# Head attention: maxima in two-row transfers, scans that lead by 24, and the first heads' positions inside the first blocks

## The chip, the core and the metric
The kernel runs on one core of a Trainium2 chip. The metric is the device time of one execution in microseconds, as the median of several runs. The engines are TensorE (PE: matmuls, with PEld for weight loads), VectorE (DVE), ScalarE (ACT), GpSimd (POOL) and SyncE (SP, which only issues transfers here).

## What is computed
The reference is a "macaron" block on 4096 tokens of 256 features, x of shape (2, 2048, 256):

```python
x = x + 0.5 * ffn(layernorm(x))     # three tree-routed feed-forwards, then attention over them
x = x + att(layernorm(x))           # 16 heads, what this change is about
x = x + 0.5 * ffn(layernorm(x))
# att, with 32 groups n = (batch, head slice), each 2048 rows of d_head 16:
att = softmax(einsum('nqd,nkd->nqk', qm, km))
att_out = einsum('nqk,nkd->nqd', att + batch_pos, vm)   # batch_pos: a relative bias table per head
```

So attention here has two products with the values: one with the softmax, one with `batch_pos`, which depends only on the head and the distance of the positions.

## The kernel before
The program is a row of stages. Those of head attention are `head_project` (q, k, v and their parts), `head_attend` (which the change is in) and `head_close`.

`head_attend` works through 32 blocks (BLOCKS), a block being one batch and head slice of 2048 rows. A block has two units (u = 2n and 2n + 1), each for half of the queries. A unit has 16 steps (RC), c = 0 to 15.

*Scans.* To know each query's maximum before the exponential, TensorE first computes all scores of a unit with queries as rows (`scan`, 32 matmuls of 48x512 a unit, into four PSUM banks `s1_ps`). VectorE takes maxima over two of them at once (`scan_max`), then forms the negative maximum of each query, splits it in two float32r parts (a cast and a subtraction) and transposes them (`max_parts`, four pieces put behind the first four scan maxima of the next unit). SP copies the transposed rows into the two last rows of the query stack `qs` (`load_m`), so that the score matmul subtracts the maximum itself.

*Scores.* `score` computes scores with keys as rows (50x512, the 50 being 48 rows and the two parts), ScalarE takes the exponential from PSUM (three turns of `s2_ps`, counted in `turn_of`), and `products` multiplies them by the values two steps (LATE) later. The ones column in the values gives the sum of the softmax.

*Order.* TensorE's order is written out in `step`: in each step two scans and two scores alternate, then follow the eight matmuls of `products`. The scans run ahead of the scores by one unit less four scans: LEAD is 14 steps of two, 28 scans, so a unit's last scans are made in step c = 1 of the unit before it. Before the first step stand all 32 scans of unit 0 and 28 of unit 1, with no other work beside them.

*Turn.* At the end of block n, VectorE transposes the block's output from PSUM and takes reciprocals of the sums (`turn_out`, in its own order behind scan maximum `TURN_AT` of an odd unit); TensorE waits for that before it writes `o_ps` again. On this GpSimd starts `finish`: it multiplies by the reciprocal, adds the position part and stores the block; then it issues the next loads (`load_pos`, `load_v`), places the values (`place_v`), and prepares a head two ahead (`prepare_above` in even, `prepare_below` in odd blocks: one 128x512 multiply, 15 small dependent adds, then casts and subtractions).

*Positions.* `positions(h, half)` is a burst of 11 matmuls for a head, in a turn of `s2_ps`; ScalarE copies it out (`copy_positions`), SP stores it (`store_pos`) and GpSimd loads it back for `finish`. Head 0 is done in the prologue, between scans of unit 1; head h + 1 in the second step (POS_AT = 1) of the even units of head h's blocks.

*Waits.* Each step of a unit that begins waits for `m_loaded` (all its `load_m` transfers), a block's first for its loads and for `v_placed`.

Of the kernel before, what the change touches and what calls it, by code (L numbers as in the profile page):

```python
# [34 lines left out]
PARTS = 2  # L35
# [1183 lines left out]
def head_attend(nc, tag, stacks, scan_loaded, ones_set, parts_d, v_d, table_d, skew_d, pos_d, att_d):  # L1219
# [3 lines left out]
    with ExitStack() as ctx:  # L1223
# [17 lines left out]
        UNIT = RC * PAIR  # L1241
        SCANS = UC * QG
        RING = 2 * SLOTS
        LEAD, LATE = 14, 2
        BANKS, TURNS = 4, 3
        QUADS = P // COLS
        HALF = 512 // 2
# [42 lines left out]
        stored = sem("att_stored")  # L1290
        LOADS = 2 * TERMS
        HEAD_LOADS = 3 + B
        MLOADS = QUADS * PARTS
        MSTEPS = 3
        FSTEPS = 2
        BELOW_STEPS, ABOVE_STEPS = RC + 4, RC + 5
        SUMS = BELOW_STEPS + ABOVE_STEPS

        turn_of = {}
        for half in range(2):  # L1300
            turn_of["pos", 0, half] = len(turn_of)
        for n in range(BLOCKS):
            for u in (2 * n, 2 * n + 1):
                for c in range(RC):
                    for g in range(PAIR):
                        turn_of["score", u, PAIR * c + g] = len(turn_of)
                    if c == POS_AT and u % 2 == 0 and n // 2 + 1 < HEADS:
                        turn_of["pos", n // 2 + 1, n % 2] = len(turn_of)

        def scores_done(n):  # L1310
            return turn_of["score", 2 * n + 1, UNIT - 1] + 1
# [15 lines left out]
        def _(sp):  # L1327
            def load_m(u):
                k = u // 2 % SLOTS
                sp.wait_ge(mT_made, u + 1)  # L1330
                for i in range(QUADS):
                    for part in range(PARTS):
                        row = LOW + QKROWS + part
                        at = i * COLS + part * UC
                        sp.dma_start(qs[row:row + 1, k, half_of(u), i * COLS:(i + 1) * COLS].bitcast(F32),
                                     mT[at:at + UC, u % 2, :]).then_inc(m_loaded, 16)

            def skew(h):
                sp.dma_start(skew_d[h], table_d[h:h + 1, :].broadcast_to([P, TABLE])).then_inc(skewed, 16)
# [24 lines left out]
            load_head(1)  # L1364
            load_m(0)
            load_head(2)
            for half in range(2):
                store_pos(0, half)
            for n in range(BLOCKS):
                if n > 0:  # L1370
                    sp.wait_ge(s2_made, scores_done(n - 1))
                if n + 2 < BLOCKS:
                    load_qk(sp, parts_d, stacks, n + 2, 0, scan_loaded)
                if n // 2 + 1 < HEADS:
                    store_pos(n // 2 + 1, n % 2)
                load_m(2 * n + 1)
                if n + 2 < BLOCKS:
                    load_qk(sp, parts_d, stacks, n + 2, LOW, score_loaded)
                if n % 2 == 0 and n // 2 + SLOTS < HEADS:
                    load_head(n // 2 + SLOTS)  # L1380
                    if n // 2 + SLOTS + 1 < HEADS:
                        skew(n // 2 + SLOTS + 1)
                if n + 1 < BLOCKS:
                    load_m(2 * n + 2)
            for k in range(2):
# [3 lines left out]
        def _(pool):  # L1389
# [75 lines left out]
            prepare_below(1)  # L1465
            prepare_above(1)
            prepare_below(2)
            load_pos(0)
            for n in range(BLOCKS):
                if n + 2 < BLOCKS:  # L1470
                    pool.wait_ge(v_placed, n + 1)
                    load_v(n + 2)
                if n + 1 < BLOCKS:
                    if n > 0:
                        pool.wait_ge(o_made, n)
                    place_v(n + 1)
                ahead = (n + 5) // 2
                if ahead < HEADS:
                    (prepare_below, prepare_above)[(n + 1) % 2](ahead)
                finish(n)  # L1480
                if n + 1 < BLOCKS:
                    load_pos(n + 1)
# [3 lines left out]
        def _(pe):  # L1486
# [52 lines left out]
            def step(u):  # L1539
# [5 lines left out]
                for c in range(RC):  # L1545
                    ahead = PAIR * (c + LEAD)
                    to, e = u + 1 + ahead // SCANS, ahead % SCANS
                    if to % 2 == 0 and e == 0 and to < UNITS:
                        pe.wait_ge(scan_loaded[to // 2 % SLOTS], 16 * LOADS * (to // 2 // SLOTS + 1))
                    for k in range(PAIR):  # L1550
                        if to < UNITS:
                            scan(to, e + k)
                        score(u, c, k)
                    if c >= LATE:
                        if c == LATE and u % 2 == 0 and n > 0:
                            pe.wait_ge(turn_step, 2 * n - 1)
                        products(u, c - LATE)
                    elif u > 0:
                        products(u - 1, RC + c - LATE)
                    if c == POS_AT and u % 2 == 0 and n // 2 + 1 < HEADS:  # L1560
                        positions(n // 2 + 1, n % 2)

            pe.wait_ge(scan_loaded[0], 16 * LOADS)
            for e in range(SCANS):
                scan(0, e)
            pe.wait_ge(constants_set, 4)
            for e in range(LEAD * PAIR):
                if e in (8, 16):
                    positions(0, e // 8 - 1)
                scan(1, e)  # L1570
            for u in range(UNITS):
                step(u)
# [57 lines left out]
        def _(act):  # L1630
# [6 lines left out]
                nc.scalar.copy(pos[:, half, groups, :].rearrange("p g w -> p (g w)"),  # L1637
                               s2_ps[:, turn % TURNS, 0:RC * W // 2]).then_inc(s2_free, 1)

            for half in range(2):  # L1640
                copy_positions(0, half)
            for u in range(UNITS):
                n = u // 2
                for i in range(UNIT):
# [2 lines left out]
                    act.wait_ge(s2_made, turn + 1)  # L1647
                    nc.scalar.activation(probs[:, (RC * u + c) % (LATE + 1), 4 * g:4 * g + 4, :].rearrange("p c t -> p (c t)"),  # L1648
                                         s2_ps[:, turn % TURNS, :], ACT.Exp).then_inc(s2_free, 1)
                    if c == POS_AT and g == PAIR - 1 and u % 2 == 0 and n // 2 + 1 < HEADS:  # L1650
                        copy_positions(n // 2 + 1, n % 2)


def head_close(nc, tag, w, att_d, y_d, x_in, x_out):
# [425 lines left out]
```

## Time and profile before

| | |
|---|---|
| median of 3 runs | 3017.08 us (3011.81 to 3024.38) |
| the profiled execution, its own time | 3022.94 us |
| its span, first to last instruction | 3021.1 us |
| TensorE busy in the span | 2805.2 us (93%) |
| VectorE busy | 2143.6 us (71%) |
| ScalarE busy | 1800.7 us (60%) |
| GpSimd busy | 801.5 us (27%) |
| mean granted TensorE clock | 0.961 |
| head attention, first scan to last product | 808 to 2174 us |

The busy shares are over all stages, which have different limits. A busy TensorE is not one at its peak, since the ends of matmuls are modelled. Times in the timelines count from the start of the span. "Idle before" is how long the engine stood still before a group, with the one that released it. In the trace the PSUM tiles s1_ps and s2_ps are both shown as `s_ps_ha`: line 1492 is the scan, line 1504 the score, line 1529 the positions.

### The profile page before, as it was taken

Reading aid. Unit: us, or ns where it says so; the run is one execution under the profiler, and the core shown is the slowest. Engines: PE = TensorE matmul, PEld = TensorE weight load, DVE = VectorE, ACT = ScalarE, POOL = GpSimd, SP = SyncE. Lnnn points to the kernel's source line nnn. Section 1 sums busy time; section 2 is a strip of 40 time slices with the busy share of each in tenths; the row PEclk is TensorE's granted clock in tenths of the full one; section 3 lists DMA queues with packets and bytes.
Section 4 is the critical chain, followed back from the end, with each engine's and each line's share of the span. In section 5 each row is a group of like instructions: output and inputs, shape, how many; then the busy total and the mean of one; then the engine's idle time right before and its main releaser. Section 6 shows DMA issues by size and latency. Waiting matters only on the chain. (4 is left out here: it accounts for less than half of the span.)

```text
span 3021.1 us, 57357 instructions
## 1 busy us (share of the span) xinstructions
PE 2805.2 (93%) x21096; PEld 1725.5 (57%) x21096; DVE 2143.6 (71%) x3412; ACT 1800.7 (60%) x3507; POOL 801.5 (27%) x1290
## 2 busy tenths in 40 slices
PE   4998999998799999999999999999786699899999
PEld 2877888886543333333333333333253377788888
DVE  5545555445589999999999999999344555555554
ACT  3445343335268888888888888888633355443333
POOL 4652300002352233322333222300012564320000
PEclk8999999998789999999999999999997799999999
DMA  8994211106954454454555454442043699221100
GB/s 261 292 303 126 67 31 32 32 23 221 263 68 61 59 69 63 55 67 58 63 68 68 59 66 53 55 57 33 13 158 113 187 306 304 74 60 32 32 27 21
DMA packets 442366, 302.17 MB, mean 100 GB/s; under 512 B 167768, under 2 KB 418748, under 8 KB 442092
## 3 DMA queue, kind: packets, MB, share of 16 engines
q1 hardware_dynamic: 413292, 214.59, 34.9%
q0 software_dynamic: 28800, 83.92, 8.9%
q8 instruction: 173, 2.83, 0.4%
q14 instruction: 101, 0.83, 0.1%
HBM read 183.27 MB, written 118.78 MB: 100 GB/s over the span
## 5 line engine op out<-in xcount | busy, mean ns | idle before, releaser
L1581 DVE TENSOR_REDUCE mx_ha<-s_ps_ha 128x2 f32<-128x1024 f32 x1024 | 1237.8, 1219 | 32.0 <-PE s_ps_ha L1492 27.3
L1648 ACT ACTIVATE probs_ha<-s_ps_ha 128x512 f32<-128x512 f32 x2048 | 1111.7, 595 | 169.0 <-PE s_ps_ha L1504 25.1
L1492 PE MATMUL s_ps_ha<-ks_ha,qs_ha 48*128 48x512 f32 x2048 | 760.7, 452 | 23.9 <-DVE mx_ha L1581 14.2
L1504 PE MATMUL s_ps_ha<-qs_ha,ks_ha 50*128 50x512 f32 x2048 | 747.9, 445 | 0.0
L1513 PE MATMUL o_ps_ha<-probs_ha,vs_ha 128*32 128x256 f32 x8192 | 654.1, 391 | 1.4 <-DVE oT_ha L1609 1.4
L1492 PEld LDWEIGHTS s_ps_ha<-ks_ha,qs_ha 48*128 48x128 f32 x2048 | 308.4, 188 | 444.9 <-DVE mx_ha L1581 388.7
L908 ACT ACTIVATE probsT_a<-pT_ps_a 128x512 fp32r<-128x512 f32 x256 | 146.3, 597 | 422.6 <-PE pT_ps_a L778 422.6
L1513 PEld LDWEIGHTS o_ps_ha<-probs_ha,vs_ha 128*32 128x32 f32 x8192 | 161.2, 108 | 375.6 <-ACT probs_ha L1648 352.0
L1504 PEld LDWEIGHTS s_ps_ha<-qs_ha,ks_ha 50*128 50x128 f32 x2048 | 302.0, 185 | 12.4 <-ACT probs_ha L1648 11.9
L1444 POOL TENSOR_TENSOR onorm_ha<-oT_ha,rinv_ha 128x256 f32<-128x256 f32 x32 | 19.9, 623 | 929.8 <-DVE rinv_ha L1612 929.8
L821 DVE TENSOR_REDUCE nmax_a<-s_ps_a 128x1 f32<-128x2048 f32 x64 | 146.7, 2292 | 155.3 <-PE s_ps_a L767 155.3
L728 POOL DMA_INDIRECT rows_a<-ys_d,slots x96 | 90.7, 945 | 620.0 <-PE turn_ps_a L750 572.1
L449 DVE COPY y_p<-y_ps_p 128x256 f32<-128x256 f32 x282 | 119.5, 424 | 190.2 <-PE y_ps_p L591 152.1
L253 POOL DMA_INDIRECT xs_d<-xn_p,row_of_p x192 | 186.2, 970 | 165.9 <-PE xT_ps_p L555 68.9
L481 ACT ACTIVATE h_p<-h_ps_p,wa_p 65x128 f32<-65x128 f32 x282 | 102.3, 363 | 170.8 <-PE h_ps_p L581 166.9
L767 PE MATMUL s_ps_a<-k0T_a,qT_a 128*128 128x512 f32 x768 | 202.2, 408 | 0.0
L581 PE MATMUL h_ps_p<-xsT_p,wa_p 128*65 128x128 f32 x1128 | 175.3, 278 | 25.2 <-issue 19.9
L767 PE MATMUL s_ps_a<-k1T,qT_a 128*128 128x512 f32 x768 | 190.4, 398 | 0.0
L800 PE MATMUL o_ps_a<-v_a,probsT_a 128*128 128x512 f32 x512 | 188.8, 408 | 0.0
L800 PE MATMUL o_ps_a<-v,probsT_a 128*128 128x512 f32 x512 | 188.5, 408 | 0.0
L581 PEld LDWEIGHTS h_ps_p<-xsT_p,wa_p 128*65 128x65 f32 x1128 | 134.6, 139 | 70.7 <-issue 37.9
L591 PE MATMUL y_ps_p<-leaf_w_p,h_p 65*128 x564 | 171.7, 386 | 0.6 <-issue 0.5
(221 smaller groups left out, 3884.0 us busy)
## 6 DMA issues: line engine op xcount, KB each, us to landing
xs_p<-xs_d SPq DMA_DIRECT2D x282, 128.0 KB
ys_d<-y_p SPq DMA_DIRECT2D x66, 512.0 KB
qs_ha<-parts_d SPq DMA_DIRECT2D x192, 128.0 KB, 4.5
ks_ha<-parts_d SPq DMA_DIRECT2D x192, 128.0 KB, 5.1
parts_d<-parts_hp POOLq DMA_DIRECT2D x32, 512.0 KB, 7.6
qs_ha<-mT_ha SPq DMA_DIRECT2D x512, 1.0 KB
xs_d<-y_p SPq DMA_DIRECT2D x6, 1024.0 KB, 12.4
leaf_w_p<-in_wa SPq DMA_DIRECT2D x4, 1048.0 KB
```

Of the source, the lines that this page charges most:

```text
L253: pool.indirect_dma_start(xs_d[f], bass.IndirectOffsetOnAxis(row_of[:, f, t:t + 1], 0), xn[:, t, :], None).then_inc(scattered[f], 16)
L581: last = nc.tensor.matmul(h_ps[0:W1C, n % 2, 0:P], wa[:, n % WB, c * W1C:(c + 1) * W1C], xsT[:, n % 2, c, :], start=(c == 0), stop=(c == C ...
L591: nc.tensor.matmul(y_ps[:, n % 2, 0:D], h[:, n % 2], leaf_w[0:W1C, n // SEG % 2, bass.ds(at + LA, D)], start=True, stop=True).then_inc(y_m ...
L767: last = nc.tensor.matmul(s_ps[:, g, :], qT[:, i % 2, hq, c, :], kT[b][:, hk, c, g * 512:(g + 1) * 512], start=(c == 0 and n == 0), stop=( ...
L800: nc.tensor.matmul(o_ps[:, :], probsT[:, 0, g, k * P:(k + 1) * P], value.rearrange("p h d -> p (h d)"), start=first, stop=False)
L821: nc.vector.reduce_max(nmax[:, :], s_ps[:, :, :].rearrange("p a b -> p (a b)"), AX_X, negate=True).then_inc(max_done, 1)
L908: nc.scalar.activation(probsT[:, 0, g, :], pT_ps[:, g % 2, :], ACT.Identity).then_inc(pT_high, 1)
L1492: nc.tensor.matmul(s1_ps[:, e % BANKS, :], qs[0:QKROWS, k, c, :], ks[0:QKROWS, k, g * 4:(g + 1) * 4, :].rearrange("p c t -> p (c t)"), sta ...
L1504: nc.tensor.matmul(out, ks[LOW:LOW + KR, k, c, :], qs[LOW:LOW + KR, k, first:first + 4, :].rearrange("p c t -> p (c t)"), start=True, stop ...
L1513: last = nc.tensor.matmul(out, vs[:, u // 2 % SLOTS, c, :], probs[:, (RC * u + c) % (LATE + 1), :, i * COLS:(i + 1) * COLS], start=(c == 0 ...
L1581: nc.vector.reduce_max(mx[:, at:at + 2], s1_ps[:, e % BANKS:e % BANKS + 2, :], AX_X).then_inc(s1_free, 1)
L1648: nc.scalar.activation(probs[:, (RC * u + c) % (LATE + 1), 4 * g:4 * g + 4, :].rearrange("p c t -> p (c t)"), s2_ps[:, turn % TURNS, :], A ...
```

## The change
LEAD goes from 14 to 12, so that scans lead by 24: 24 scans of unit 1 stand in the prologue, and a unit's last scans are made in step c = 3 of the unit before. `TURN_AT`, which is computed from it, goes from 30 to 26. `load_m` copies both parts of a quadrant in one transfer of two rows (16 source partitions), four in place of eight. The positions of head 0 leave the prologue; `pos_of` puts head 0 in units 0 and 1, head 1 in units 2 and 3, and the later heads where they were. SP stores the position halves in that order, and GpSimd's `load_pos(0)` comes behind its first preparations in block 0.

```diff
--- before.py
+++ after.py
@@ -1241,7 +1241,7 @@
         UNIT = RC * PAIR
         SCANS = UC * QG
         RING = 2 * SLOTS
-        LEAD, LATE = 14, 2
+        LEAD, LATE = 12, 2
         BANKS, TURNS = 4, 3
         QUADS = P // COLS
         HALF = 512 // 2
@@ -1290,22 +1290,25 @@
         stored = sem("att_stored")
         LOADS = 2 * TERMS
         HEAD_LOADS = 3 + B
-        MLOADS = QUADS * PARTS
+        MLOADS = QUADS
         MSTEPS = 3
         FSTEPS = 2
         BELOW_STEPS, ABOVE_STEPS = RC + 4, RC + 5
         SUMS = BELOW_STEPS + ABOVE_STEPS
 
+        def pos_of(u):
+            if u < 4:
+                return u // 2, u % 2
+            return (u // 4 + 1, u // 2 % 2) if u % 2 == 0 and u // 4 + 1 < HEADS else None
+
         turn_of = {}
-        for half in range(2):
-            turn_of["pos", 0, half] = len(turn_of)
         for n in range(BLOCKS):
             for u in (2 * n, 2 * n + 1):
                 for c in range(RC):
                     for g in range(PAIR):
                         turn_of["score", u, PAIR * c + g] = len(turn_of)
-                    if c == POS_AT and u % 2 == 0 and n // 2 + 1 < HEADS:
-                        turn_of["pos", n // 2 + 1, n % 2] = len(turn_of)
+                    if c == POS_AT and pos_of(u):
+                        turn_of["pos", *pos_of(u)] = len(turn_of)
 
         def scores_done(n):
             return turn_of["score", 2 * n + 1, UNIT - 1] + 1
@@ -1328,12 +1331,11 @@
             def load_m(u):
                 k = u // 2 % SLOTS
                 sp.wait_ge(mT_made, u + 1)
+                row = LOW + QKROWS
                 for i in range(QUADS):
-                    for part in range(PARTS):
-                        row = LOW + QKROWS + part
-                        at = i * COLS + part * UC
-                        sp.dma_start(qs[row:row + 1, k, half_of(u), i * COLS:(i + 1) * COLS].bitcast(F32),
-                                     mT[at:at + UC, u % 2, :]).then_inc(m_loaded, 16)
+                    at = i * COLS
+                    sp.dma_start(qs[row:row + PARTS, k, half_of(u), i * COLS:(i + 1) * COLS].bitcast(F32),
+                                 mT[at:at + PARTS * UC, u % 2, :]).then_inc(m_loaded, 16)
 
             def skew(h):
                 sp.dma_start(skew_d[h], table_d[h:h + 1, :].broadcast_to([P, TABLE])).then_inc(skewed, 16)
@@ -1364,15 +1366,13 @@
             load_head(1)
             load_m(0)
             load_head(2)
-            for half in range(2):
-                store_pos(0, half)
             for n in range(BLOCKS):
                 if n > 0:
                     sp.wait_ge(s2_made, scores_done(n - 1))
                 if n + 2 < BLOCKS:
                     load_qk(sp, parts_d, stacks, n + 2, 0, scan_loaded)
-                if n // 2 + 1 < HEADS:
-                    store_pos(n // 2 + 1, n % 2)
+                if pos_of(2 * n):
+                    store_pos(*pos_of(2 * n))
                 load_m(2 * n + 1)
                 if n + 2 < BLOCKS:
                     load_qk(sp, parts_d, stacks, n + 2, LOW, score_loaded)
@@ -1380,6 +1380,8 @@
                     load_head(n // 2 + SLOTS)
                     if n // 2 + SLOTS + 1 < HEADS:
                         skew(n // 2 + SLOTS + 1)
+                if pos_of(2 * n + 1):
+                    store_pos(*pos_of(2 * n + 1))
                 if n + 1 < BLOCKS:
                     load_m(2 * n + 2)
             for k in range(2):
@@ -1465,7 +1467,6 @@
             prepare_below(1)
             prepare_above(1)
             prepare_below(2)
-            load_pos(0)
             for n in range(BLOCKS):
                 if n + 2 < BLOCKS:
                     pool.wait_ge(v_placed, n + 1)
@@ -1477,6 +1478,8 @@
                 ahead = (n + 5) // 2
                 if ahead < HEADS:
                     (prepare_below, prepare_above)[(n + 1) % 2](ahead)
+                if n == 0:
+                    load_pos(0)
                 finish(n)
                 if n + 1 < BLOCKS:
                     load_pos(n + 1)
@@ -1557,16 +1560,14 @@
                         products(u, c - LATE)
                     elif u > 0:
                         products(u - 1, RC + c - LATE)
-                    if c == POS_AT and u % 2 == 0 and n // 2 + 1 < HEADS:
-                        positions(n // 2 + 1, n % 2)
+                    if c == POS_AT and pos_of(u):
+                        positions(*pos_of(u))
 
             pe.wait_ge(scan_loaded[0], 16 * LOADS)
             for e in range(SCANS):
                 scan(0, e)
             pe.wait_ge(constants_set, 4)
             for e in range(LEAD * PAIR):
-                if e in (8, 16):
-                    positions(0, e // 8 - 1)
                 scan(1, e)
             for u in range(UNITS):
                 step(u)
@@ -1637,8 +1638,6 @@
                 nc.scalar.copy(pos[:, half, groups, :].rearrange("p g w -> p (g w)"),
                                s2_ps[:, turn % TURNS, 0:RC * W // 2]).then_inc(s2_free, 1)
 
-            for half in range(2):
-                copy_positions(0, half)
             for u in range(UNITS):
                 n = u // 2
                 for i in range(UNIT):
@@ -1647,8 +1646,8 @@
                     act.wait_ge(s2_made, turn + 1)
                     nc.scalar.activation(probs[:, (RC * u + c) % (LATE + 1), 4 * g:4 * g + 4, :].rearrange("p c t -> p (c t)"),
                                          s2_ps[:, turn % TURNS, :], ACT.Exp).then_inc(s2_free, 1)
-                    if c == POS_AT and g == PAIR - 1 and u % 2 == 0 and n // 2 + 1 < HEADS:
-                        copy_positions(n // 2 + 1, n % 2)
+                    if c == POS_AT and g == PAIR - 1 and pos_of(u):
+                        copy_positions(*pos_of(u))
 
 
 def head_close(nc, tag, w, att_d, y_d, x_in, x_out):
```

## Rows read from the trace of the kernel before

**Rows 1.** Timeline of TensorE in an ordinary block: start us, duration us, engine, line, operands.
```profile
1599.75 1.31 PE L1529 MATMUL s_ps_ha<-vpp_ha,bandp_ha 128*128 128x256 f32 x9
1601.23 0.49 PE L1492 MATMUL s_ps_ha<-ks_ha,qs_ha 48*128 48x512 f32 x1
1601.89 0.64 PE L1513 MATMUL o_ps_ha<-probs_ha,vs_ha 128*32 128x256 f32 x8
...
1606.82 0.64 PE L1513 MATMUL o_ps_ha<-probs_ha,vs_ha 128*32 128x256 f32 x8
1608.53 0.64 PE L1513 MATMUL o_ps_ha<-probs_ha,vs_ha 128*32 128x256 f32 x8
...
1618.97 0.50 PE L1504 MATMUL s_ps_ha<-qs_ha,ks_ha 50*128 50x512 f32 x1
```

**Rows 2.** The page's costliest groups, the exponentials: busy us, mean ns | idle before.
```profile
L1648 ACT ACTIVATE probs_ha<-s_ps_ha 128x512 f32<-128x512 f32 x2048 | 1111.7, 595 | 169.0 <-PE s_ps_ha L1504 25.1
```

**Rows 3.** Timeline of VectorE and GpSimd in the same block.
```profile
1604.34 0.55 POOL L1391 DMA_DIRECT2D vflat_ha<-vh_d  x1
1604.37 0.57 DVE L1592 CAST mparts_ha<-nmax_ha 128x8 fp32r<-128x8 f32 x1
1604.85 1.21 DVE L1581 TENSOR_REDUCE mx_ha<-s_ps_ha 128x2 f32<-128x1024 f32 x1
1605.59 1.05 POOL L1412 TENSOR_TENSOR above_ha<-vp_ha,far_ha 128x512 f32<-128x512 f32 x1
1605.99 0.69 DVE L1595 TENSOR_TENSOR mparts_ha<-nmax_ha,mparts_ha 128x8 fp32r<-128x8 f32 x1
1606.72 4.87 POOL L1416 TENSOR_TENSOR above_ha<-above_ha 128x32 f32<-128x32 f32 x15
```

**Rows 4.** Groups of max_parts on VectorE: duration ns min/median/max.
```profile
L1588 DVE TENSOR_REDUCE nmax_ha<-mx_ha x64: 129/175/178, 830.7 to 2136.9; 128x8 f32<-128x32 f32 x64
L1592 DVE CAST mparts_ha<-nmax_ha x64: 159/163/580, 831.9 to 2137.0; 128x8 fp32r<-128x8 f32 x64
L1595 DVE TENSOR_TENSOR mparts_ha<-nmax_ha,mparts_ha x64: 149/157/1230, 833.5 to 2137.2; 128x8 fp32r<-128x8 f32 x64
```

**Rows 5.** Timeline, block beginnings early and late; then GpSimd's groups, 900 to 2100 us.
```profile
1601.50 0.62 POOL L1444 TENSOR_TENSOR onorm_ha<-oT_ha,rinv_ha 128x256 f32<-128x256 f32 x1 [27.87 <-DVE rinv_ha L1612]
...
1642.91 0.62 POOL L1444 TENSOR_TENSOR onorm_ha<-oT_ha,rinv_ha 128x256 f32<-128x256 f32 x1 [27.84 <-DVE rinv_ha L1612]
...
2014.92 0.62 POOL L1444 TENSOR_TENSOR onorm_ha<-oT_ha,rinv_ha 128x256 f32<-128x256 f32 x1 [36.79 <-DVE rinv_ha L1612]
...
2017.79 0.58 DVE L1592 CAST mparts_ha<-nmax_ha 128x8 fp32r<-128x8 f32 x1
2019.41 0.15 DVE L1595 TENSOR_TENSOR mparts_ha<-nmax_ha,mparts_ha 128x8 fp32r<-128x8 f32 x1
...
2055.86 0.62 POOL L1444 TENSOR_TENSOR onorm_ha<-oT_ha,rinv_ha 128x256 f32<-128x256 f32 x1 [36.80 <-DVE rinv_ha L1612]
...
L1412 POOL TENSOR_TENSOR below_ha<-vp_ha,far_ha 128x512 f32<-128x512 f32 x13 | 13.7, 1051 | 0.0
```

**Rows 6.** Windows: us, busy us of each engine, granted clock (PEclk), DMA share, GB/s.
```profile
856.00:857.00 1.00, 1.00 (x7) 0.55 (x6) 0.00 (x0) 0.37 (x1) 0.77 (x4) 0.74 0.00 0
```

**Rows 7.** Timeline of TensorE, prologue of head attention.
```profile
830.79 2.44 PE L1492 MATMUL s_ps_ha<-ks_ha,qs_ha 48*128 48x512 f32 x4 [0.25 <-DVE mx_ha L1581]
...
836.46 2.07 PE L1492 MATMUL s_ps_ha<-ks_ha,qs_ha 48*128 48x512 f32 x4
...
838.99 2.35 PE L1492 MATMUL s_ps_ha<-ks_ha,qs_ha 48*128 48x512 f32 x4 [0.46 <-DVE mx_ha L1581]
...
851.61 0.76 PE L1492 MATMUL s_ps_ha<-ks_ha,qs_ha 48*128 48x512 f32 x1 [0.28 <-DVE mx_ha L1581]
```

**Rows 8.** Timeline of SP's queue; then the page's DMA issues: KB, us to landing.
```profile
835.06 5.53 SPq L1335 DMA_DIRECT2D qs_ha<-mT_ha  x8
...
qs_ha<-parts_d SPq DMA_DIRECT2D x192, 128.0 KB, 4.5
```

## Prediction

> **What bounds the kernel now.** I read the page first for shares, then the windows, then the timeline of head attention (808 to 2175 us), where every edit lies. The question there is which engine sets the length of a step. In this stage one step of TensorE (`c` in `step`) makes two scans beside two scores and then eight product matmuls. The reader is to see that product bursts follow each other at 4.93 us for four steps, 1.233 us a step [rows 1]. Nothing else fills a step: two exponentials of 0.595 us are 1.19 us [rows 2], and VectorE, where it has fallen behind, needs 1.14 us for a scan maximum (it starts at 1604.85 and the next instruction at 1605.99) [rows 3]. So TensorE sets the pace, ScalarE is 0.04 us behind it and VectorE has 0.09 us of slack a step. Shortening VectorE's work is worth something only where VectorE falls so far behind that TensorE finds no free bank.
>
> That place exists. In an ordinary block one step takes 1.71 us (1606.82 to 1608.53), 0.48 us over [rows 1]. Just before it VectorE ran late: the cast took 0.57 us and the subtraction 0.69 us, against medians of 0.163 and 0.157 us [rows 3, 4]. Both ended as a GpSimd instruction ended: the cast with the v transfer's issue (1604.34 + 0.55 = 1604.89), the subtraction with the 128x512 multiply (1605.59 + 1.05 = 1606.64) [rows 3]. They are the only two that wait: the maximum over `mx` never exceeds 178 ns in 64 [rows 4]. They meet GpSimd because `turn_out` stands after the last pair of a unit, so the work GpSimd starts on `rinv` runs beside the next unit's `max_parts`.
>
> A control lies in the same trace. In late blocks no head is prepared any more; the cast still takes 0.58 us, the subtraction 0.15 us, and the block is 2055.86 - 2014.92 = 40.94 us long instead of 1642.91 - 1601.50 = 41.41 us [rows 5]. So one wait of about 0.4 us is absorbed by the two pairs of scan banks, and two (some 0.9 us) cost TensorE 0.47 us.
>
> The Trainium skill (SBUF, State Buffer, section Who interferes with whom) says that VectorE and GpSimd share a port pair as an exclusive lock for a whole instruction, that a two-port cast and a two-input `tensor_tensor` take part, and that `tensor_reduce` on trn2 does not. The trace agrees: the cast and the subtraction reach 580 and 1230 ns, the reduction 178 [rows 4]. By that rule each VectorE instruction waits for one GpSimd instruction, whichever started first.
>
> **The change part by part.**
>
> *Lead 24 in place of 28, prologue.* Four scans leave the prologue. There the clock is granted at half (1.2 GHz; it crosses in the row of 856 to 857 us at 0.74) and four scans take 838.99 - 836.46 = 2.53 us [rows 6, 7]. They don't vanish, they move into steps whose 1.233 us is set by work that is there anyway; the last two steps with scans replace two without. I take -2.5 us in full. Cover gone would mean that steps without scans are shorter; ScalarE's 1.19 us allows no more than 2 x 0.04 us of that [rows 2].
>
> *Positions of head 0 out of the prologue.* From the scans at 830.79 to the first step at 851.61 is 20.82 us; six groups of four scans are 15.18 us; the 5.64 us left are the two position products at half clock and a wait for `distantp` [rows 7]. VectorE idles meanwhile, so all of it goes: -5.6 us. ScalarE's table load, which stood behind the copy, is then before the first step.
>
> *Positions inside blocks.* Before, units 0 and 2 carried head 1. After, units 0 and 1 carry head 0, units 2 and 3 head 1: two bursts more in steps. Unit 0's burst is there either way, at half clock. A burst at full clock takes TensorE 1601.23 - 1599.75 = 1.48 us, and nothing lies under it [rows 1]: +3.0 us for units 1 and 3. On the other side, if the turn of o_ps in units 0 or 2 had been hiding part of it, this is unchanged there.
>
> *`TURN_AT` 30 to 26.* It follows from the lead. TensorE's step is the same (c = 1), so the wait for `turn_step` stays. But two scan maxima now stand between `turn_out` and the next unit. Count from the start of GpSimd's chain, which follows `rinv` (1601.50 in the block shown). VectorE then takes pairs 28, 30 and 0 at TensorE's pace, the maximum over `mx`, pair 2, and comes to the cast two steps (2.47 us) later than before, near +5.3 us, and to the subtraction near +6.6 us. GpSimd's chain is unmoved: its transfers end at +3.4 us, the big multiply at +5.1 us, and the 15 adds of 4.87 us start at +5.2 us, 0.325 us apart [rows 3, 5]. So both now fall among adds, each waiting at most one add. Bounds: 0 and 2 x 0.32 us a block. Either is below what the two pairs of banks absorbed in the control (0.4 us), or barely over it. I take no stall, since the cast's own wait will be 0.1 to 0.25 us. The multiply of `prepare_below` occurs 13 times between 900 and 2100 us [rows 5], that of `prepare_above` as often: 26 blocks, each with 0.475 us: -12.4 us. By the skill's lock, which lets the later one in when the earlier instruction ends, the sum is the same.
>
> *Transfers of the maxima.* Eight one-row transfers cost SP 5.53 us, 0.69 us each [rows 8]; four are 2.8 us. With twice the elements each, the far end is the same transfers at twice the issue, 1.38 us each and 5.5 us in all, as before; that is the upper bound. I take 2.8 us, since the count of descriptors has no row that shows it in the issue. No score waits for the maxima in the waits of before. The path: the transposed maxima are ready about 2.5 us later, near +8.0 us (1609.5); the next unit's first score is at 1618.97, or 1618.5 without the stall [rows 1]. That leaves 9.0 us, minus 2.8 us of issue, 6.2 us for landing (3.5 us at the upper bound). The row for landing nearest in kind is 4.5 us for 128 KB [rows 8]; 1 or 2 KB should not be worse. Cost 0; both ends: 0, or 5.5 + 4.5 - 9.0 = 1.0 us in each of 64 halves. The issues removed lie on SP, which waits for VectorE anyhow, so no gain.
> The Trainium skill (DMA: Bandwidth & Descriptors, section on the SWDGE path) gives about 2.0 us fixed for a transfer; no row here shows the landing of these, and by it they land with 4 us to spare.
>
> *SP and GpSimd order.* `store_pos(h, 1)` for heads 0 and 1 moves behind `load_qk` and `load_head` and waits for ScalarE's copy in an odd unit's second step; behind it stands only `load_m(2n+2)`, whose maxima come six steps later. The next copy, which needs these stores, is 16 steps (19.7 us) later; cover is ample. GpSimd's `load_pos(0)` waits for the second store before `finish(0)`, which waits anyway until `turn_out(0)` in unit 2's time. Cost 0; if the store took all its cover plus 4 us, a few us once.
>
> **Sum.** -2.5 - 5.6 + 3.0 - 12.4 = -17.5 us. Profiled execution: 3022.9 us (span 3021.1, 1.8 around it) becomes 3005.4. The median of the runs is 5.9 us below the profiled one, 3017.08: 2999.5 us, 0.58% less.
>
> **Rivals.**
> A, the forecast: 2999.5, own range 2994 to 3006.
> B, the collisions only change partner: two waits among adds, or VectorE's start slipping by 0.2 us into the multiply, still exceed the banks' slack. For it: GpSimd is busy without a break until +10 us. Against: no add is longer than 0.25 us. Then only the prologue counts: -5.1 us, 3012.
> C, the full clock comes later. Rows: it rose 4.9 us after the dense steps began at 851.61, and the bursts of positions that stood before are gone [rows 6, 7]. A step at half clock is some 1.2 us longer; two to four more of them: +2.4 to +5 us, so 3002 to 3004.5. [...]
> D, slower: the two-row transfers land too late for the first score of a unit. It decides from 9.0 us between transpose and landing of the last; beyond it each us costs 64. At the upper bounds above, 1.0 us x 64 = 64 us minus 17.5: 3063. Against: today's eight, ready at 1607.93, issue until 1613.4 and land within the 5.6 us that are left.
>
> **Chances.** A 0.76, B 0.11, C 0.09, D 0.04. About 0.5% is what a measurement here can tell from no change: faster means below 3002.0, slower above 3032.2. A lies only 2.5 us under the line, so I give it 0.54 faster and 0.22 same; C 0.04 and 0.05; B is same; D slower. Together 0.58, 0.38, 0.04. The range goes from 2992 (the medians scatter; the three runs of before span 12.6 us) to 3013 (B).
>
> **What the profile would show.** Right: first step near 843.5 us; every block of the middle 40.9 us long instead of 41.4, no 1.71 us step; cast and subtraction each under 0.45 us in odd units; bursts of positions in units 0 to 3, 1.48 us each; no wait on the maxima. Wrong: a cast or subtraction over 0.5 us again and a long step behind it (B); half clock beyond 849 us (C); scores waiting for a transfer at each unit's start (D).

## The result, and the profile after

The changed kernel takes 3001.01 us (median of 5 runs, 2997.15 to 3004.72), the kernel before 3017.08 us (median of 5, 3011.81 to 3024.38). The ratio is 0.9939, 95% interval 0.9923 to 0.9956: faster by 13 to 23 us. Forecast were 2999.5 us, the range 2992 to 3013, and 0.58 for faster by over 0.5%.

The profiled execution took 3004.72 us, its span is 3002.9 us, 18.2 us less than before. That is close to the forecast 17.5 us, but not by the forecast's terms alone. Head attention runs from the first scan to the last turn of `o_ps` (groups: duration min/median/max in ns, then first and last start in us; in the changed code the scan is line 1495, the score 1507, the product 1516, the position matmul 1532):

```profile
L1495 PE MATMUL s_ps_ha<-ks_ha,qs_ha x2048: 392/493/794, 802.2 to 2120.7; 48*128 48x512 f32 x187
L1610 DVE STREAM_TRANSPOSE oT_ha<-o_ps_ha x32: 704/706/716, 890.4 to 2157.1; 128x512 f32<-128x512 f32 x32
```

From 802.2 to 2157.1 are 1354.9 us. Before it was 808.0 to 2174.0, 1366.0 us. So this one profile shows 11.1 us won in head attention, 5.8 us in stages ahead of it whose code is the same, and 1.3 us behind it. The 5.8 us are a difference between two executions, not a term of the change: in the twelve other profiles below, whose code ahead of head attention is the same too, the first scan starts anywhere from 820.6 to 830.1 us. The medians still differ by 16 us; the second profile of the changed kernel, below, fits that, with 1349.6 us for head attention.

**The long step.** The timeline of VectorE and GpSimd in a block, and TensorE's products in it:

```profile
1588.73 0.62 POOL L1446 TENSOR_TENSOR onorm_ha<-oT_ha,rinv_ha 128x256 f32<-128x256 f32 x1 [27.35 <-DVE rinv_ha L1613]
...
1591.56 0.55 POOL L1393 DMA_DIRECT2D vflat_ha<-vh_d  x1
...
1592.82 1.05 POOL L1414 TENSOR_TENSOR above_ha<-vp_ha,far_ha 128x512 f32<-128x512 f32 x1
1593.94 4.86 POOL L1418 TENSOR_TENSOR above_ha<-above_ha 128x32 f32<-128x32 f32 x15
...
1594.06 0.16 DVE L1593 CAST mparts_ha<-nmax_ha 128x8 fp32r<-128x8 f32 x1
...
1595.30 0.24 DVE L1596 TENSOR_TENSOR mparts_ha<-nmax_ha,mparts_ha 128x8 fp32r<-128x8 f32 x1
...
1594.05 0.64 PE L1516 MATMUL o_ps_ha<-probs_ha,vs_ha 128*32 128x256 f32 x8
1595.28 0.64 PE L1516 MATMUL o_ps_ha<-probs_ha,vs_ha 128*32 128x256 f32 x8
1596.52 0.64 PE L1516 MATMUL o_ps_ha<-probs_ha,vs_ha 128*32 128x256 f32 x8
...
1629.67 0.62 POOL L1446 TENSOR_TENSOR onorm_ha<-oT_ha,rinv_ha 128x256 f32<-128x256 f32 x1 [27.39 <-DVE rinv_ha L1613]
```

The reader is to see that GpSimd's chain stands as before relative to its first instruction, the multiply by `rinv` (v transfer at +2.83 us, multiply at +4.09 us; before +2.84 and +4.09 [rows 3, 5]) while the cast has moved to +5.33 and the subtraction to +6.57 us. They take 0.16 and 0.24 us where they took 0.57 and 0.69 [rows 3]. The products keep their 1.23 us, and the block is 1629.67 - 1588.73 = 40.94 us, the length that before only the blocks without preparation had [rows 5]. Over all 64 halves:

```profile
L1593 DVE CAST mparts_ha<-nmax_ha x64: 159/161/173, 826.1 to 2122.6; 128x8 fp32r<-128x8 f32 x64
L1596 DVE TENSOR_TENSOR mparts_ha<-nmax_ha,mparts_ha x64: 155/156/689, 827.4 to 2122.8; 128x8 fp32r<-128x8 f32 x64
```

The cast's maximum fell from 580 to 173 ns [rows 4]. The subtraction's 689 ns stand in the prologue, at 827.43; from the first step on it never exceeds 256 ns. All 26 steps with 0.48 us too much are gone.

**The prologue and the clock.** TensorE's timeline, first score to the return of the full clock, then two windows with the granted clock (PEclk) third from the end:

```profile
838.23 0.79 PE L1507 MATMUL s_ps_ha<-qs_ha,ks_ha 50*128 50x512 f32 x1
...
840.59 2.29 PE L1532 MATMUL s_ps_ha<-vpp_ha,bandp_ha 128*128 128x256 f32 x9
...
844.39 1.08 PE L1516 MATMUL o_ps_ha<-probs_ha,vs_ha 128*32 128x256 f32 x8
...
846.54 1.08 PE L1516 MATMUL o_ps_ha<-probs_ha,vs_ha 128*32 128x256 f32 x8
...
855.18 1.07 PE L1516 MATMUL o_ps_ha<-probs_ha,vs_ha 128*32 128x256 f32 x8
...
856.85 0.64 PE L1516 MATMUL o_ps_ha<-probs_ha,vs_ha 128*32 128x256 f32 x8
```

```profile
855.00:856.00 1.00, 1.00 (x10) 0.20 (x8) 0.71 (x1) 0.98 (x2) 0.92 (x3) 0.50 0.00 0
856.00:857.00 1.00, 1.00 (x12) 0.45 (x12) 0.69 (x3) 0.25 (x1) 1.00 (x1) 0.95 0.00 0
```

The first score comes 838.23 - 802.18 = 36.05 us after the first scan (before 851.61 - 807.95 = 43.66), 7.6 us sooner. But the clock stays at 1.2 GHz until 856.1 (0.95 granted in the row of 856 to 857), 17.9 us after the first score, where it had taken 4.9 us [rows 6, 7]. From one product burst to the next, five steps take some 2.16 us (the first 844.39 to 846.54) and one 1.67, in place of 1.23 us: 5 x 0.93 + 0.44 = 5.1 us.

**The transfers.** SP's timeline and the group of all two-row transfers, then the group of the one-row transfers before:

```profile
829.40 2.83 SPq L1337 DMA_DIRECT2D qs_ha<-mT_ha  x4
```

```profile
L1337 SPq DMA_DIRECT2D qs_ha<-mT_ha x256: 596/607/801, 829.4 to 2125.3; - x128
```

```profile
L1335 SPq DMA_DIRECT2D qs_ha<-mT_ha x512: 623/626/1470, 835.1 to 2142.7; - x171
```

Four take 2.83 us where eight took 5.53 us [rows 8]; the issue of two rows costs SP no more than that of one (medians 0.607 and 0.626 us). No first score waits for them: the first of each unit comes at least 6.0 us after the last issue.

### The profile page after: what moved, and what is told of

The parts are those of the page before. It is cut to its first block and busy times, and to the rows that moved or that the text cites. A ratio compares the mean times of both kernels' runs of the same rounds, so it can differ in the third digit from the quotient of the medians.

```text
span 3002.9 us, 57103 instructions
## 1 busy us (share of the span) xinstructions
PE 2800.4 (93%) x21096; PEld 1720.9 (57%) x21096; DVE 2130.2 (71%) x3412; ACT 1800.3 (60%) x3507; POOL 801.8 (27%) x1290
## 3 DMA queue, kind: packets, MB, share of 16 engines
q8 instruction: 173, 2.83, 0.4%
## 5 line engine op out<-in xcount | busy, mean ns | idle before, releaser
L1495 PE MATMUL s_ps_ha<-ks_ha,qs_ha 48*128 48x512 f32 x2048 | 764.5, 454 | 11.1 <-PEq L952 7.9
L1507 PEld LDWEIGHTS s_ps_ha<-qs_ha,ks_ha 50*128 50x128 f32 x2048 | 303.7, 186 | 11.5 <-ACT probs_ha L1647 11.1
```

Source lines behind the costliest of these rows:

```text
L1495: nc.tensor.matmul(s1_ps[:, e % BANKS, :], qs[0:QKROWS, k, c, :], ks[0:QKROWS, k, g * 4:(g + 1) * 4, :].rearrange("p c t -> p (c t)"), sta ...
L1507: nc.tensor.matmul(out, ks[LOW:LOW + KR, k, c, :], qs[LOW:LOW + KR, k, first:first + 4, :].rearrange("p c t -> p (c t)"), start=True, stop ...
```

## The experiments

These ran on other chips of the same kind, where the kernel before takes 3065 to 3069 us. So the ratio to it on the same chip counts, and beside it the length of head attention in the profile, first scan to last turn, since it leaves out what the other stages do. For the kernel before that length is from one profile, on the first chip; e4_rows, which has its order, takes 1367.8 us on another. The last column is the time from the first score to the full clock, in the one profile that each row has.

| kernel | ratio (95%) | head attention us | clock us |
|---|---|---|---|
| before | 1 | 1366.0 | 4.9 |
| changed | 0.9939 (0.9923 to 0.9956) | 1354.9 | 17.9 |
| e1_shift | 0.9958 (0.9920 to 0.9996) | 1354.5 | 5.3 |
| e2_pos | 0.9980 (0.9955 to 1.0004) | 1364.0 | 5.6 |
| e3_lead | 0.9973 (0.9957 to 0.9989) | 1354.5 | 8.2 |
| e4_rows | 1.0003 (0.9988 to 1.0019) | 1367.8 | 5.8 |
| e5_again | 0.9944 (0.9923 to 0.9965) | 1349.6 | 5.0 |
| e6_both | 0.9940 (0.9921 to 0.9959) | 1350.2 | 7.3 |
| e7_lead10 | 0.9930 (0.9911 to 0.9948) | 1346.8 | 5.7 |
| e8_lead8 | 0.9950 (0.9932 to 0.9968) | 1356.1 | 15.5 |
| e9_both10 | 0.9941 (0.9922 to 0.9960) | 1347.2 | 6.1 |
| e10_pad | 0.9970 (0.9952 to 0.9988) | 1358.3 | 7.1 |
| e11_both9 | 0.9946 (0.9928 to 0.9963) | 1350.2 | 7.2 |
| e12_late | 0.9950 (0.9934 to 0.9966) | 1351.8 | 11.2 |

### Is the long step GpSimd's doing? e1_shift and e10_pad

e1_shift is the kernel before; it leaves the lead and `TURN_AT` alone and moves `max_parts` (an excerpt):

```diff
-                    if u > 0 and e // 2 <= MSTEPS:
-                        max_parts(u - 1, e // 2)
+                    if u > 0 and 2 <= e // 2 <= MSTEPS + 2:
+                        max_parts(u - 1, e // 2 - 2)
```

> The kernel before with one edit: the four pieces of max_parts stand behind scan maxima 4, 6, 8 and 10 of the next unit in place of 0, 2, 4 and 6, so that they come two steps later, as a shorter lead makes them. Lead, positions and transfers as before. Theory of the two waits on GpSimd: the cast and the subtraction leave the v transfer's issue and the 128x512 multiply, no step of 1.71 us is left, blocks are 40.9 us long, about -12.4 us (ratio near 0.996). Rival, that the shorter lead itself (scans earlier in the banks' order) removed the long step: blocks stay at 41.4 us and the time stays within 2 us of before.

Head attention is 11.5 us shorter, and none of the 26 steps is left; blocks are 40.9 us long. One step of 1.75 us, at 881.85 in the first block, is another: there the cast (0.48 us) and the subtraction (0.81 us) wait for the end of GpSimd's first preparations and for its placing of the values. Over the steps longer than 1.3 us, position bursts included, the excess over 1.233 us sums to 44.8 us against 56.9 us, 12.0 us less. Neither a shorter lead nor another place of `turn_out` is needed for the gain.

e10_pad is the reverse. It keeps the changed kernel's order and holds GpSimd up (an excerpt; a scratch tile and a semaphore are added):

```diff
                 finish(n)
+                if n > 0:
+                    pool.wait_ge(padded, 4 * n)
+                for i in range(3):
+                    nc.gpsimd.tensor_tensor(scratch[:, i], unit[:, :, :], unit[:, :, :], ALU.mult).then_inc(padded, 1)
+                nc.gpsimd.tensor_copy(scratch[:, 3], unit[:, :, :]).then_inc(padded, 1)
                 if n + 1 < BLOCKS:
                     load_pos(n + 1)
```

> The changed kernel with four GpSimd instructions on a scratch tile (three 128x256 multiplies and a copy, some 2.5 us in all) between the block's store and the next loads; nothing else moves. It is the reverse of shifting max_parts: lead, transfers and VectorE's order stay as changed, but GpSimd's v transfer issue and 128x512 multiply come 2.5 us later, where the cast and the subtraction now stand. Theory of the two waits: the cast takes some 0.5 us and the subtraction 0.6 us again, 26 steps of about 1.7 us come back, 12 us more than the changed kernel, ratio 0.998. Rival, that the shorter lead or the order of turn_out removed the long steps: GpSimd's extra 2.5 us in 41 are hidden, ratio 0.994 as the changed kernel.

The four instructions moved GpSimd's chain by 2.1 us in place of 2.5. The timeline of VectorE and GpSimd, then of TensorE:

```profile
1616.62 0.57 POOL L1399 DMA_DIRECT2D posn_ha<-pos_d  x1
1617.18 0.54 POOL L1395 DMA_DIRECT2D vflat_ha<-vh_d  x1
1617.73 0.75 POOL L1403 TENSOR_TENSOR vs_ha<-vflat_ha,unit_ha 128x256 f32<-128x256 f32 x1
1618.43 1.05 POOL L1416 TENSOR_TENSOR above_ha<-vp_ha,far_ha 128x512 f32<-128x512 f32 x1
...
1617.59 0.94 DVE L1600 CAST mparts_ha<-nmax_ha 128x8 fp32r<-128x8 f32 x1
...
1619.57 0.15 DVE L1603 TENSOR_TENSOR mparts_ha<-nmax_ha,mparts_ha 128x8 fp32r<-128x8 f32 x1
```

```profile
1619.70 0.49 PE L1502 MATMUL s_ps_ha<-ks_ha,qs_ha 48*128 48x512 f32 x1 [0.26 <-DVE mx_ha L1589]
```

The same wait of a scan for VectorE's maximum stood in the long step of before; ahead of it the placing of the values, which there came behind the cast:

```profile
1604.90 0.74 POOL L1399 TENSOR_TENSOR vs_ha<-vflat_ha,unit_ha 128x256 f32<-128x256 f32 x1
...
1607.87 0.49 PE L1492 MATMUL s_ps_ha<-ks_ha,qs_ha 48*128 48x512 f32 x1 [0.41 <-DVE mx_ha L1581]
```

The cast now takes 0.94 us, until the placing of the values ends (1617.73 + 0.75 = 1618.48), and the subtraction is just past the multiply. In each prepared block one step takes 1.56 us, 0.33 us too much; the 26 sum to 8.5 us, and head attention is 1358.3 - 1349.6 = 8.7 us longer than in the changed kernel with an early clock (e5_again, below). The forecast of 12 us was missed because the shift was smaller and only one of the two instructions met a long one; the mechanism came back on demand. It also corrects the wording of the forecast: one wait is enough if it is long. What counts is the sum, here some 0.8 us and 0.9 us before. Less the excess of the step, 0.33 and 0.48 us, both leave some 0.45 us that the scan banks hold, an estimate from these two.

### What the other parts do: e2_pos, e3_lead, e4_rows

e2_pos is the changed kernel with LEAD at 14 and eight one-row transfers.

> The kernel before with the positions' part alone: head 0 in units 0 and 1, head 1 in units 2 and 3; lead 28 and eight transfers as before. Sum of the prediction: 5.6 us off the prologue, two bursts of 1.48 us more, -2.6 us, and the 26 long steps of 1.71 us stay. If the bursts in the prologue are what brings the full clock early, its rise comes some 10 us or more after the first step in place of 4.9 us, which gives back 3 to 6 us: about +1 to +3 us in all. If the rise comes at a time that has nothing to do with the bursts, it can be anywhere and differs from profile to profile.

Head attention is 2.0 us shorter (forecast 2.6), the first score 38.4 us after the first scan in place of 43.7. The cast's and the subtraction's maxima are those of before, 573 and 1230 ns, and the 26 long steps stand. The clock is not late although no burst of positions is left in the prologue:

```profile
868.48 0.79 PE L1508 MATMUL s_ps_ha<-qs_ha,ks_ha 50*128 50x512 f32 x1
...
874.00:875.00 1.00, 1.00 (x14) 0.19 (x10) 0.49 (x1) 0.68 (x2) 0.92 (x2) 0.96 0.42 37
```

It is full from 874.1, 5.6 us after the first score. The bursts in the prologue are thus not needed for an early clock.

e3_lead changes LEAD and nothing else.

```diff
-        LEAD, LATE = 14, 2
+        LEAD, LATE = 12, 2
```

> The kernel before with the lead alone at 24 scans (turn_out goes behind pair 26 with it); head 0's positions in the prologue and eight one-row transfers as before. Theory: -2.5 us of prologue and -12.4 us of the long steps, -14.9 us, ratio near 0.995. The transfers are issued until 5.5 us after the transpose, and 3.5 us are left for the last to land: if they land later than that, each unit's first score waits and the gain is less. Clock: with the bursts in the prologue it rises within 5 us of the first step, if the bursts are what brings it.

The 26 long steps are gone, but head attention is 11.5 us shorter, not 14.9. The timeline shows a wait that the forecast for this kernel missed:

```profile
869.84 2.29 PE L1529 MATMUL s_ps_ha<-vpp_ha,bandp_ha 128*128 128x256 f32 x9 [2.01 <-POOL distantp_ha L1405]
```

With the positions still in the old order, unit 0 multiplies head 1, whose sums GpSimd finishes at 868.53 + 1.26 = 869.8. The shorter lead brings TensorE there 2.0 us too soon. The positions part of the change puts head 0 there, whose sums have long been done. So the two parts depend on each other: most of the lead's 2.5 us of prologue is had only with the new order of heads. The clock, at 8.2 us, was also later than the 5 us expected, although both bursts stood in the prologue.

e4_rows makes the two-row transfers alone.

> The kernel before with the two-row transfers alone. Theory: nobody waits for the maxima, so nothing changes (ratio 0.998 to 1.002), SP's issue takes 2.8 us in place of 5.5 us. Rival: the transfers or their issue disturb the other loads or GpSimd, then the time moves by more than 5 us. Its clock should rise as that of before, 4.9 us after the first step, if the rise follows from the work in front of it.

Ratio 1.0003, 0.9988 to 1.0019: nothing, as forecast. Head attention in its profile is 1.8 us longer. Of that 1.1 us are two steps of 1.62 and 1.92 us from 875.88 on, behind a cast of 1.00 and a subtraction of 0.86 us that wait for GpSimd's first preparations, as in e1_shift.

### How early must the maxima be? e7_lead10 and e8_lead8

Both are the changed kernel with another LEAD (10 and 8).

> The changed kernel with LEAD at 10, 20 scans in place of 24. Prologue: 2.5 us less, if the two-row transfers of the maxima land in time; transposed maxima are then ready 6.6 us before the first score of their unit, issue takes 2.6 us, so 4.0 us are left for landing. GpSimd is still among its 15 adds at the cast (+7.8 us) and the subtraction (+9.0 us): no long step. If the transfers land later than 4.0 us each unit's first step waits for the rest, 64 times.

> The changed kernel with LEAD at 8, 16 scans. This is meant to make the rival of late maxima true and so to measure their landing: ready 4.1 us before the first score, 2.6 us of issue, 1.5 us left. If landing takes 2 us (what the skill's page on DMA gives as fixed), each unit starts 0.5 us late, 64 x 0.5 = 32 us slower than the changed kernel less 5 us of prologue; if it takes 4.5 us as the 128 KB loads do, 3 us late, about 190 us slower. The subtraction then falls on GpSimd's next 1.0 us instruction, which may cost up to 0.5 us a block as well.

LEAD 10 has no wait for the maxima and no long step, and head attention is 2.8 us shorter than in e5_again (forecast 2.5). In the whole kernel that is a thousandth, which the ratios don't separate. LEAD 8 gives the landing. SP's issue, and the first weights of a unit that wait for it:

```profile
920.46 2.55 SPq L1337 DMA_DIRECT2D qs_ha<-mT_ha  x4
924.09 0.18 PEld L1495 LDWEIGHTS s_ps_ha<-ks_ha,qs_ha 48*128 48x128 f32 x1 [0.44 <-DMA qs_ha<-mT_ha]
```

The last issue ends at 923.01, the weights are loaded from 924.09 on: the transfer has landed 1.1 us after its issue. In 26 odd units this distance is 1.08 to 1.13 us and the step grows by 0.01 to 0.06 us; in the even ones the first score comes 1.34 us or more after the issue, and all but two of their steps stay at 1.23 us. Of the 0.44 us of idle time 0.41 us stand before an ordinary step's first weight load too. All that the steps at a unit's start grow by adds up to some 2 us over the 64 units. Both expectations, 32 and 190 us, were far too high. Rival D needed more than 9.0 us from transpose to landing; measured are 2.55 + 1.1 = 3.7 us. What LEAD 8 does lose is the other thing: in every second block a step of 1.54 to 1.56 us, because the cast (not the subtraction, as expected) meets the 128x384 addition that follows the adds of `prepare_above` and takes up to 0.94 us; and in this profile a late clock.

### What brings the full clock? e5_again, e6_both, e12_late

e5_again is the changed kernel without an edit.

> The changed kernel once more, unaltered, on the chip of this call, for a second look at when the full clock comes. In its first profile it came 18 us after the first score (838.23 to 856.2), and six steps of unit 0 took 2.16 us in place of 1.23, 5.1 us in all; in the four profiles with a lead of 28 it came within 5.9 us, right behind the position burst of unit 0. Theory, the point in time is a matter of where the burst of 2.6 us falls against the chip's own watch of the engine: a second profile shows another delay, 5 to 17 us, and without the slow steps head attention is 5 us shorter. Rival, the shorter prologue itself makes it late: 17 to 18 us again.

```profile
861.00:862.00 1.00, 1.00 (x7) 0.78 (x7) 0.00 (x0) 0.06 (x1) 0.77 (x4) 0.58 1.07 108
```

The first score is at 856.82 and the clock full from 861.84: 5.0 us, no step of 2.16 us, head attention 1349.6 us, 5.3 us less than in the first profile. So the late clock does not come with the change each time; one execution had it and another had not. 1366.0 - 1349.6 = 16.4 us is what the change is worth with the clock early in both, from one profile of each.

e6_both returns both bursts of head 0 for unit 0, and none for unit 1 (an excerpt; the loops over the list follow from it):

```diff
         def pos_of(u):
+            if u < 2:
+                return [(0, 0), (0, 1)] if u == 0 else []
             if u < 4:
-                return u // 2, u % 2
+                return [(u // 2, u % 2)]
```

> The changed kernel with both position bursts of head 0 in the second step of unit 0, one behind the other (5.3 us of 128-row matmuls at half clock), and none in unit 1. If dense 128-row work is what brings the full clock, it is there within 6 us of the first score whenever the burst falls, and no step of 2.16 us is left: 5 us less than a profile of the changed kernel with late clock, plus at most 1.2 us because the second burst runs at half clock; about 1 us slower than one with early clock. If the bursts have nothing to do with it, the clock comes as late as in the changed kernel.

```profile
864.34 2.29 PE L1534 MATMUL s_ps_ha<-vpp_ha,bandp_ha 128*128 128x256 f32 x9
...
866.86 2.10 PE L1534 MATMUL s_ps_ha<-vpp_ha,bandp_ha 128*128 128x256 f32 x9
...
869.34 0.50 PE L1509 MATMUL s_ps_ha<-qs_ha,ks_ha 50*128 50x512 f32 x1
```

Both bursts passed at half clock; it was full from 869.3, 0.4 us behind the second (the scores take 0.50 us). That is 7.3 us after the first score where under 6 were expected, and head attention is 0.6 us longer than in e5_again where about 1 us was; both of one profile.

e12_late is e6_both with `u == 1` in the first line: no burst in unit 0.

> The changed kernel with both position bursts of head 0 in the second step of unit 1 and none in unit 0, so that only scans (48 rows), scores (50 rows) and products stand in unit 0. In all profiles so far but two, the full clock came at the end of, or within a step or two of, the burst in unit 0; in those two (17.8 and 15.5 us after the first score) the burst had passed without it. If a dense 128-row burst is what usually brings it, it comes late here, 15 us or more after the first score, with five or more steps of unit 0 at 2.16 us, 5 us or more of head attention against the second profile of the changed kernel (1349.6 us from the first scan to the last turn), less 1.4 us because the burst of unit 0 at half clock is gone. If steady scans, scores and products are enough, it comes within 8 us and head attention is 1 to 2 us shorter.

```profile
873.00:874.00 1.00, 1.00 (x8) 0.32 (x10) 0.16 (x2) 0.51 (x2) 0.86 (x2) 0.50 0.00 0
874.00:875.00 1.00, 1.00 (x10) 0.22 (x4) 1.00 (x1) 0.57 (x2) 0.77 (x4) 0.61 0.00 0
```

It came 11.2 us after the first score at 863.63, between the two expectations, and head attention is 2.2 us longer than in e5_again. Here only scans, scores and products ran in unit 0 before the clock rose, so a burst of 128 rows is not the only thing that it can follow. Why two profiles with one burst in unit 0 show 17.9 and 15.5 us and the others with one 4.9 to 8.2 us stays open: the changed kernel did both.

### A better version? e9_both10 and e11_both9

They join LEAD 10 or 9 with both bursts in unit 0.

> A version that should beat both: the changed kernel with LEAD 10 (20 scans) and both position bursts of head 0 in unit 0. Against the changed kernel 2.5 us less prologue; the full clock within 8 us of the first score in every run, where with one burst it came after 5 us in some profiles and after 16 to 18 us in others (5 us dearer); 1.2 us more for the second burst at half clock. Ratio 0.992 to 0.993. If the clock still comes late, the burst is not what brings it.

> The same with LEAD 9 (18 scans). 1.27 us less prologue again. Maxima: ready 5.35 us before the first score, 2.6 us of issue, 2.7 us for landing; with LEAD 8 they had 1.5 us and 33 first scores waited 0.46 us on average, so landing takes up to 2 us or a little more and nobody should wait here but for single cases. The subtraction comes at +10.3 us, on GpSimd's next 1.0 us instruction: one wait a block, which the scan banks absorb (under 0.45 us). Ratio 0.992; if waits on the maxima are left, 0.993 or more.

e9_both10 has an early clock (6.1 us) and head attention of 1347.2 us, 3.0 us less than e6_both; its ratio, 0.9941, is not below that of the changed kernel, where 0.992 to 0.993 was expected. In e11_both9 head attention is 3.0 us longer again: in every second block the subtraction meets the same addition, and a step of 1.57 us follows. The timeline of VectorE and GpSimd:

```profile
1615.69 0.94 DVE L1598 TENSOR_TENSOR mparts_ha<-nmax_ha,mparts_ha 128x8 fp32r<-128x8 f32 x1
...
1615.61 1.01 POOL L1437 TENSOR_TENSOR distant_ha<-below_ha,above_ha 128x384 f32<-128x384 f32 x1
```

They end at 1616.63 and 1616.62. The expectation that one such wait is absorbed was wrong for the reason seen in e10_pad. No version clearly beats the changed kernel; by the profiles LEAD 10 is 2.4 to 2.8 us shorter, less than the runs can tell.

## Why the prediction was right

- *TensorE sets the pace.* Right: with 26 stalls gone the ordinary step is 1.23 us, no shorter, in every kernel here.
- *The long steps, -12.4 us.* Right in size and place: none is left, 12.0 us less excess in e1_shift, and e10_pad brings them back in part. The forecast of 0.1 to 0.25 us for a wait among the adds was a little high: 0.16 and 0.24 us in all, against 0.16 us free. "Two waits" was the wrong count; the sum of the waits against some 0.45 us is what the runs bear out: in e11_both9 a single wait of 0.79 us gives a step of 1.58 us.
- *Prologue, -2.5 and -5.6 us.* First scan to first score is 36.05 and 36.2 us in the two profiles, against 43.7: -7.5 us where -8.1 stood. In e2_pos the positions alone gave 5.2 us where 5.6 stood; profiles with the same prologue differ by up to 0.4 us, so the rest can't be placed. The first step, forecast near 843.5 us, came at 838.23; 5.8 us of that lie ahead of the stage.
- *Two bursts more, +3.0 us.* Right: 31 steps of 2.71 us in place of 29, each 1.48 us over.
- *Transfers, nothing.* Right, with far more room than thought: landing was taken from the row of 128 KB loads, 4.5 us, and is 1.1 us.
- *The sum, -17.5 us.* Measured in head attention: 16.4 us with the clock early in both, 11.1 us in the first profile. The measured terms add up to -7.5 - 12.5 + 3.0 = -17.0; the 0.6 us between were not traced.
- *Rival C* held in that one profile, together with A and not in its place. It cost 5.1 us, the top of the 2.4 to 5 us written, but by other terms: a step at half clock is 0.93 us longer and not 1.2, and there were five and a part where two to four were thought of. Its reason, that the bursts are gone from the prologue, fell with e2_pos and e5_again. It should have stood as a spread on every case and not as a case.
- The agreement of 2999.5 and 3001.0 us is partly luck: the executions of one kernel spread over 8 to 13 us. Much of that can lie where the change doesn't reach: over the twelve later profiles the stages ahead of head attention differ by up to 9.4 us and those behind it by up to 8.8 us.

## What to carry to other kernels

An engine with a tenth of a microsecond of slack a step can still cost time where its small instructions meet another engine's long ones and wait for them; look for casts and two-input instructions whose maximum is several times their median, and see which instruction's end ends them. Moving them by two steps won 12 us here, more than the 7.5 us taken out of the prologue. A shorter lead is safe as long as two other things are counted: the landing (measure it by shrinking the lead until a wait shows) and the work that the earlier start meets unprepared, as head 1's sums in e3_lead.

## What the runs showed of the hardware that was not expected

- A VectorE cast can wait through more than one GpSimd instruction: in e10_pad it started 0.41 us into a v transfer's issue and ended with the placing of the values behind it, 0.94 us in all. In the kernel before the cast started 0.03 us into the same issue and ended with it [rows 3], and the placing of the values followed at 1604.90. The Trainium skill (SBUF, State Buffer, section Who interferes with whom) has the later one block until the earlier ends; the second instruction that slipped in between is not explained by it, nor by a run here.
- The cast took 0.16 us at 1594.06, inside an add that by its row had begun at 1593.94. GpSimd's spans are rough, so whether short adds block at all stays open; in the changed kernel's blocks they cost at most 0.1 us (the subtraction's 256 against 156 ns).
- TensorE stayed at half clock for 17.9 us with scans, scores and products following almost without a gap (busy 17.87 us of 838.2 to 856.1), and the same kernel had full clock after 5.0 us in another execution. The prologue ahead of it was not sparse either: from 802.2 to 838.2 us TensorE was busy 32.9 of 36.0 us, all at half clock. The Trainium skill (TensorE: Matmul & The Clock Gate, part 1) says that activity releases the throttle. In both profiles the clock rose behind the busy steps, as it says; what made it 17.9 us in one and 5.0 us in the other, no run shows.
- A transfer of 2 KB between two places in SBUF, issued by SP, landed 1.1 us after its issue ended. The Trainium skill (DMA: Bandwidth & Descriptors, section on the SWDGE path) gives some 2.0 us fixed, for transfers that GpSimd issues; the measured value is less, 1.7 us even with the 0.6 us of its own issue.
